# One layer on one core: attention scores from 32-bit terms in two halves of the array, in blocks of 2048 queries

## What is computed

```
xn  = layernorm(x)
q,k,v = xn @ Wq.T + bq, xn @ Wk.T + bk, xn @ Wv.T + bv     # 16 heads of 16
scores = (q * 16**-0.5) @ k.T                              # per batch and head: 4096 x 4096
attn = softmax(scores) @ v ;  attn @ Wo.T + bo
ffn(xn): 8 experts of width 256, silu(xn@Wg)*(xn@Wu) @ Wd, weighted by a router
out = x + attention + ffn
```

## Time and profile before

| | us |
|---|---|
| median of three launches | 7797.84 (7790.06 to 7806.21) |
| the profiled launch, span | 7797.1 |
| setup and tokens | 0 to 1378 |
| attention, first load to last column | 1378 to 7698 |
| output | 7699 to 7797 |

### The profile page before, as it was taken

How to read it: one execution, slowest core, us unless ns; L and a number is a source line. 1 busy time by engine, 2 the same in 40 slices (tenths; PEclk the granted TensorE clock), 3 DMA queues, 4 the chain that set the end, 5 groups by cost and what they waited for, 6 DMA issues and landing times. The chain is left out here.

```text
span 7797.1 us, 144290 instructions
## 1 busy us (share of the span) xinstructions
PE 7608.5 (98%) x42896; PEld 3174.4 (41%) x42896; DVE 5806.7 (74%) x7413; ACT 5255.3 (67%) x9557; POOL 542.1 (7%) x543
## 2 busy tenths in 40 slices
PE   7999999899999999999999999999999999999998
PEld 6888888233333333333333333333333333333334
DVE  5455454788787878787878787878787878787884
ACT  3333333577777777777777777777777777777774
POOL 2433333000000000000000000000000000000000
PEclk9999999899999999999999999999999999999999
DMA  2111110200000000000000000000000000000002
GB/s 75 42 42 34 41 42 28 62 8 8 8 8 8 8 8 8 8 8 8 8 8 8 8 8 8 8 8 8 8 8 8 8 8 8 8 8 8 8 0 86
DMA packets 97328, 135.88 MB, mean 17 GB/s; under 512 B 9824, under 2 KB 90976, under 8 KB 90976
## 3 DMA queue, kind: packets, MB, share of 16 engines
q1 hardware_dynamic: 97120, 133.48, 7.8%
HBM read 83.11 MB, written 50.33 MB: 17 GB/s over the span
## 5 line engine op out<-in xcount | busy, mean ns | idle before, releaser
L881 DVE TENSOR_REDUCE mx<-sc 128x1 f32<-128x1024 f32 x4096 | 4824.0, 1219 | 1138.4 <-PE sc L756 1138.4
L864 ACT ACTIVATE pr<-st 128x512 f32<-128x512 f32 x8160 | 4427.8, 595 | 1489.3 <-PE st L778 1375.2
L778 PE MATMUL st<-qr,kr 98*128 (+1 forms) x8160 | 2634.5, 387 | 75.3 <-ACT pr L864 51.8
L756 PE MATMUL sc<-kr,qr 96*128 (+1 forms) x8192 | 2140.5, 383 | 23.2 <-DMA kr<-parts_d 18.1
L785 PE MATMUL pv<-pr,vst 128*32 128x512 f32 x14336 | 1920.2, 608 | 0.1
L778 PEld LDWEIGHTS st<-qr,kr 98*128 98x128 bf16 x8160 | 648.6, 97 | 2469.5 <-ACT pr L864 2016.9
L756 PEld LDWEIGHTS sc<-kr,qr 96*128 (+1 forms) x8192 | 795.5, 97 | 1043.2 <-issue 141.3
L428 ACT ACTIVATE gated<-gate 128x512 f32<-128x512 f32 x256 | 152.3, 599 | 609.2 <-PE up L88 609.0
L613 DVE TENSOR_TENSOR hraw<-gated,up 128x512 f32<-128x512 f32 x256 | 173.3, 686 | 411.0 <-ACT gated L428 408.6
L785 PEld LDWEIGHTS pv<-pr,vst 128*32 128x32 f32 x14336 | 282.7, 108 | 416.9 <-issue 416.9
L724 POOL COPY vtail<-v_all 128x64 f32 (+1 forms) x32 | 7.6, 238 | 6074.8 <-PE pv L785 6074.8
(11 more groups left out here) (112 smaller groups left out, 2401.3 us busy)
## 6 DMA issues: line engine op xcount, KB each, us to landing
parts_d<-part SPq DMA_DIRECT2D x64, 384.0 KB, 2.7
qr<-parts_d SPq DMA_DIRECT2D x192, 128.0 KB, 4.3
kr<-parts_d SPq DMA_DIRECT2D x192, 128.0 KB, 7.0
x_in<-in_L_attn_hidden_states SPq DMA_DIRECT2D x16, 512.0 KB, 4.5
v_d<-v_sb SPq DMA_DIRECT2D x32, 256.0 KB, 2.1
base_d<-base SPq DMA_DIRECT2D x16, 512.0 KB, 3.2
v_all<-v_d SPq DMA_DIRECT2D x1, 8192.0 KB, 32.3
o_base<-base_d SPq DMA_DIRECT2D x16, 512.0 KB, 4.2
```

The source lines that it names most:

```text
L756: last = nc.tensor.matmul(sc[u % 2][:, j * GT:(j + 1) * GT], qr[0:ROWS, bass.ds(ring(stage) + qb * GT + t * P, P)], kr[0:ROWS, bass.ds(rin ...
L778: nc.tensor.matmul(score_bank(kb, maxima), kr[0:ROWSM, bass.ds(ring(stage) + kb * P, P)], qr[0:ROWSM, bass.ds(ring(stage) + qb * GT, GT)], ...
L864: nc.scalar.activation(pr[:, kb % PRING, :], score_bank(kb, maxima), ACT.Exp).then_inc(exp_done, 1)
L881: nc.vector.reduce_max(mx[:, odd, u // MAXU, u % MAXU:u % MAXU + 1], sc[u % 2][:, :], AX.X).then_inc(sc_read, 1)
```

## The change

**Parts.** q and k are split into two fp32r parts (high, low), not three bfloat16 ones. ACT writes the high part and DVE the low part straight from PE's bank; POOL has no part in it, and the separate full value is gone. The scale 1/4 is put into Wq in setup. `parts_d` holds float32, 512 KB a store.

**Scores.** A score is three terms (high-high, low-high, high-low), 48 rows, with two rows for the maximum 50. `load` puts the same rows at partitions 0 and at 64 of `qr` and `kr`, and two matmuls with different operands are issued behind each other, one in each half of the array: in `score_pair` two blocks of 512 queries against the same 128 keys, in `max_unit` the two halves of the 1024 keys. A load of one head is again 12 DMAs, now of 256 KB.

**Superslots.** One superslot is 2048 queries of a head (QH), 64 in all. For each of its 32 blocks of 128 keys (`kb`) PE issues two score pairs (four blocks of 128 by 512), two `max_unit` for the superslot after, and `times_v` of the block before: four float32 matmuls in the four column strips, one strip for each 512 queries. So one `kb` holds just what a quad held: 4 blocks of scores, 2 units of maxima, 4 products with v. The four strips are different queries now and need no adding. There are three banks `st` (STB), and a pair waits until the block three before its second member has been read. The maxima run a whole superslot and 16 units ahead (AHEAD).

**Maxima to rows.** Once in a superslot, after `times_v` at `kb` 26, PE transposes the 32 columns of maxima (`turned`) into a bank of `st`, ACT copies it to `mrow`, and four DMAs put it into the rows of `qr`.

**Results.** ACT copies `pv` to `oT` once in a superslot, and eight DMAs store sums and denominators, undivided and already feature by token, to `sums_d` and `den_d`. v of a head comes by one DMA from `v_d` in pieces of 16 numbers. The copies of v on POOL, `max_rows`, `out_back` and DVE's three steps after it are gone.

**Output.** The denominators are loaded, inverted by DVE and stored to `rden_d` first. Then SP issues for each group 2 loads of sums, 16 loads of one row of `rden_d` each, spread over 16 partitions, and the load of `base`. POOL multiplies the two. There are no transposes. The next group's loads wait for the store of the group before (`stored`) and for POOL (`attn_ready`).

**Loops.** The attention loop holds two heads, four superslots, written out in one body; the first and last pass stand outside it.

The diff, cut to this:

```diff
-UNITS = TPG * MAXU
-PAIRS = ((0, 0), (0, 1), (1, 0), (1, 1), (0, 2), (2, 0))
-ROWS = len(PAIRS) * HD
-ROWSM = ROWS + 2
+UNITS = QT * MAXU
+AHEAD = 16
+SUPERS = 2 * B * H
+TERMS = 3 * HD
+ROWSM = TERMS + 2
 VC = 32
-PRING = 2 * QUAD
+PRING = 16
+STB = 3
+SLOTS = KB * QSUB + 1
+ROWS_AT = 26
...
-                act.wait_ge(rest_ready, g * SPLITS + u + 1)
-                nc.scalar.activation(full[u % 2][:, :], bank[:, :], ACT.Identity, bias=bias[:, i:i + 1], scale=scale)
+                bias = c.bqs if kind == "q" else c.bk
                 act.wait_ge(parts_stored[u % 2], (g * (SPLITS // 2) + u // 2 + 1) * DMA)
-                nc.scalar.activation(part[u % 2][:, 0, :], bank[:, :], ACT.Identity, bias=bias[:, i:i + 1],
-                                     scale=scale).then_inc(misc_act, 1)
+                nc.scalar.activation(part[u % 2][:, 0, :], bank[:, :], ACT.Identity, bias=bias[:, i:i + 1]).then_inc(high_given, 1)
...
-                    dve.wait_ge(misc_act, g * MISC_ACT + emptied(n))
-                    dve.wait_ge(parts_ready, g * SPLITS + u + 1)
-                    nc.vector.tensor_tensor(rest[u % 2][:, :], full[u % 2][:, :], part[u % 2][:, 0, :],
-                                            ALU.subtract).then_inc(rest_ready, 1)
+                    bias = c.bqs if kind == "q" else c.bk
+                    dve.wait_ge(high_given, g * SPLITS + u + 1)
+                    nc.vector.scalar_tensor_tensor(out=part[u % 2][:, 1, :], in0=misc[(par * len(MISC) + n) % 2][:, :], scalar=bias[:, i:i + 1],
+                                                   in1=part[u % 2][:, 0, :].bitcast(F32), op0=ALU.add, op1=ALU.subtract).then_inc(misc_free, 1)
...
-        kr = sb("kr", [P, RING * S], BF16)
-        qr = sb("qr", [P, RING * S], BF16)
+        kr = [sb(f"kr{i}", [P, S], F32R) for i in range(RING)]
+        qr = [sb(f"qr{i}", [P, S], F32R) for i in range(RING)]
...
-        st = [pb(f"st{i}", [P, GT], F32) for i in range(2)]
+        st = [pb(f"st{i}", [P, GT], F32) for i in range(STB)]
-            load(0)
-            sp.dma_start(v_all[:, :, :], c.v_d.rearrange("(t p) d -> p t d", p=P)).then_inc(v_loaded, DMA)
-            sp.wait_ge(loaded, LOADS * DMA)
-            load(1)
-            with sp.Fori(RING, HEADS) as n:
-                wait_alone(sp, loaded, n * LOADS * DMA, passed)
-                wait_alone(sp, st_full, (n - RING + 1) * QB * KB, passed)
-                load(n)
+            def load(n, par):
+                for w, dst, order in ((0, qr, (0, 1, 0)), (1, kr, (0, 0, 1))):
+                    for grp in range(2):
+                        for term, hl in enumerate(order):
+                            r0 = 64 * grp + HD * term
+                            sp.dma_start(dst[par][r0:r0 + HD, :].bitcast(F32), c.parts_d[w, hl, bass.ds(n * HD, HD), :]).then_inc(qk_loaded, DMA)
+            def load_v(n, par):
+                sp.dma_start(vst[par][:, :, 0:HD],
+                             c.v_d[bass.ds((n // H) * S, S), bass.ds((n % H) * HD, HD)].rearrange("(t p) d -> p t d", p=P)).then_inc(v_loaded, DMA)
+            def rows(par, hf):
+                for grp in range(2):
+                    for hl in range(2):
+                        r = 64 * grp + TERMS + hl
+                        sp.dma_start(qr[par][r:r + 1, hf * QH:(hf + 1) * QH].bitcast(F32).rearrange("r (t q) -> r t q", q=P),
+                                     mrow[hl * QT:(hl + 1) * QT, :].bitcast(F32)).then_inc(rows_in, DMA)
+            def sums(s, n, hf):
+                wait_alone(sp, sums_ready, s + 2, passed)
+                for j in range(QSUB):
+                    cols = slice(hf * QH + j * GT, hf * QH + (j + 1) * GT)
+                    sp.dma_start(c.sums_d[bass.ds(n * HD, HD), cols], oT[VC * j:VC * j + HD, :]).then_inc(sums_stored, DMA)
+                    sp.dma_start(c.den_d[bass.ds(n, 1), cols], oT[VC * j + HD:VC * j + HD + 1, :]).then_inc(sums_stored, DMA)
...
-            def max_unit(n, u):
+            def max_unit(g, u, par, hf):
                 t, k = divmod(u, MAXU)
-                stage, qb = n // QB, n % QB
-                pe.wait_ge(sc_read, n * UNITS + u + 1)
-                for j in range(MAXW // GT):
-                    last = nc.tensor.matmul(sc[u % 2][:, j * GT:(j + 1) * GT],
-                                            qr[0:ROWS, bass.ds(ring(stage) + qb * GT + t * P, P)],
-                                            kr[0:ROWS, bass.ds(ring(stage) + k * MAXW + j * GT, GT)], start=True, stop=True)
+                q0 = hf * QH + t * P
+                pe.wait_ge(sc_read, g - 1 + SC_PRE)
+                for grp in range(2):
+                    r0, k0 = 64 * grp, k * MAXW + grp * GT
+                    last = nc.tensor.matmul(sc[u % 2][:, grp * GT:(grp + 1) * GT], qr[par][r0:r0 + TERMS, q0:q0 + P],
+                                            kr[par][r0:r0 + TERMS, k0:k0 + GT], start=True, stop=True)
...
-            def scores(stage, qb, kb, maxima):
-                n = (stage * QB + qb) * KB + kb
-                if maxima:
-                    pe.wait_ge(exp_done, n + 1)
-                elif qb == QB - LEAD and kb < 2:
-                    pe.wait_ge(exp_done, n + 1)
-                elif qb == QB - LEAD and kb < 4:
-                    pe.wait_ge(sc_read, HEADS * QB * UNITS + 2)
-                else:
-                    pe.wait_ge(exp_done, n - 1)
-                nc.tensor.matmul(score_bank(kb, maxima), kr[0:ROWSM, bass.ds(ring(stage) + kb * P, P)],
-                                 qr[0:ROWSM, bass.ds(ring(stage) + qb * GT, GT)], start=True, stop=True).then_inc(st_full, 1)
-            def times_v(quad, v, exps):
-                pe.wait_ge(exp_done, exps + 2)
-                for j in range(QUAD):
-                    last = nc.tensor.matmul(pv[VC * j:VC * (j + 1), :], v[:, j, :], pr[:, (quad % 2) * QUAD + j, :],
-                                            start=(quad == 0), stop=(quad == QUADS - 1))
+            def score_pair(s, kb, j0, par, hf, final):
+                x = slot_of(kb, j0, final)
+                pe.wait_ge(st_read, s * SLOTS + x + 1 - STB + 2 + READ_PRE)
+                for grp in range(2):
+                    r0, q0 = 64 * grp, hf * QH + (j0 + grp) * GT
+                    nc.tensor.matmul(st[(x + grp) % STB][:, :], kr[par][r0:r0 + ROWSM, kb * P:(kb + 1) * P],
+                                     qr[par][r0:r0 + ROWSM, q0:q0 + GT], start=True, stop=True).then_inc(st_full, 1)
+            def turned():
+                nc.tensor.transpose(st[ROWS_SLOT % STB][0:2 * QT, 0:P], nmp[:, :, :].rearrange("p h t -> p (h t)").bitcast(F32),
+                                    c.ident[:, :]).then_inc(st_full, 1)
+            def times_v(s, kb, par, final):
+                pe.wait_ge(st_read, s * SLOTS + slot_of(kb, QSUB - 1, final) + 2 + READ_PRE)
+                for j in range(QSUB):
+                    last = nc.tensor.matmul(pv[VC * j:VC * (j + 1), :], vst[par][:, kb, :], pr[:, (QSUB * kb + j) % PRING, :],
+                                            start=(kb == 0), stop=(kb == KB - 1))
...
+            for u in range(UNITS + 2):
+                max_unit(u, u % UNITS, 0, u // UNITS)
+            pe.wait_ge(max_chain, 3)
+            turned()
+            for u in range(UNITS + 2, UNITS + AHEAD):
+                max_unit(u, u % UNITS, 0, u // UNITS)
+            def body(i, first, last):
+                for q in range(PER):
+                    s, n, par, hf = PER * i + q, RING * i + q // 2, q // 2, q % 2
+                    ending = last and q // 2 == RING - 1
+                    for kb in range(KB):
+                        if kb == 0:
+                            pe.wait_ge(rows_in, (s + 1) * ROW_MOVES * DMA)
+                        if hf == 0 and not ending and 2 * kb + AHEAD == UNITS:
+                            pe.wait_ge(qk_loaded, (n + 2) * QK_LOADS * DMA)
+                        for half in range(2):
+                            score_pair(s, kb, 2 * half, par, hf, ending and hf)
+                            u = 2 * kb + AHEAD + half
+                            to = q + 1 + u // UNITS
+                            if not (last and to >= PER):
+                                max_unit(UNITS * (s + 1) + u, u % UNITS, to // 2 % RING, to % 2)
+                        if kb == 0:
+                            if not (first and q == 0):
+                                times_v(s - 1, KB - 1, par if hf else 1 - par, False)
+                            if hf == 0:
+                                pe.wait_ge(v_loaded, (n + 1) * DMA)
+                        else:
+                            if kb == 1:
+                                pe.wait_ge(sums_ready, s + 1)
+                            times_v(s, kb - 1, par, ending and hf)
+                        if kb == ROWS_AT and not (ending and hf):
+                            pe.wait_ge(max_chain, 3 * (s + 1) + 3)
+                            pe.wait_ge(st_read, s * SLOTS + ROWS_SLOT - STB + 2 + READ_PRE)
```

(79 more changed lines are left out.)

459 lines of the change are left out of this document (151 added, 308 removed).

## The result

The changed kernel took **7854.5 us** (median; 7836.2 to 7859.2) against 7798.7 for the kernel before in the same sessions: a ratio of 1.0067, with a 95% interval of 1.0053 to 1.0081. It is slower by 0.7%, where 7470 us and faster were forecast. The time is above the forecast's own 7150 to 7780 and inside the wider range to 8100, which took in a rival; the sign is wrong. The profiled launch is 7850.7 us long, 53.6 more than the one before. In a later session one of eight launches of the kernel before took 11802 us at a mean granted clock of 0.60, the others 7793 to 7801 us; the comparisons leave it out.

A forecast was written before the change was run, and what follows sets the result against it. A chain once through PE and once through ACT bounds it: 2.70 us a block for 2.88. Attention -562, opening +76, output +161, tokens -5 make -330 from 7797, say 7470 us; range 7150 to 7780, wider 7150 to 8100.

The forecast's parts named there:

- The chain's terms: Attention, one block of keys: 0.99 + 0.48 + 0.66 + 0.25 + 0.32 = 2.70 us, against 2.88 before.
- Pair to ACT: Attention chain, first score pair to ACT's exp: 0.43 plus 0.05 for the 32-bit weight load, 0.48 us.
- Second pair to the unit behind it: Attention chain, second score pair to the maxima behind it: halves run at once, so about one matmul, 0.25 us.
- rival 2: Attention: a pair's weight loads go in a row, 0.105 more for each of two pairs; block 2.90, total 7870 us; chance 0.12.
- Output: Output phase: 19 load issues a group at 0.50 us, 15.2 us a group, 259 us against 98.8: +161.
- Opening: First load to first score: fill 9, load 25, 80 units of maxima 94, in all 129 us against 52.7: +76.
- Tokens: Tokens and setup: PE stays the bound, only group 0's chain is shorter; -5 us, between -20 and +10.
- Last 40 blocks: End of attention: the last 40 blocks have no maxima, so 0.25 goes and each takes 2.45 us.
- Loop ends and superslots: Attention: pauses at 15 loop ends, 8 us each, 120; superslot extras 1.0 us x 63 = 63.
- 1 (halves not at once): Attention: the array's halves don't run at once, a pair costs 0.45, block 3.13, total 8330 us; chance 0.10.
- 3 (clock stays low): Attention: PE's clock stays at 0.50 throughout, block 4.12, +2850, total 10300 us; chance 0.04.
- 4 (DVE the bound): Attention: DVE's two reductions bound the block at 2.35 + 0.01 us, 680 less, total 6790 us; chance 0.03.

The follow-up runs named there:

- the reordered version: The changed kernel with both units of maxima between the two score pairs, instead of one between and one behind: 7335.3 us, ratio 0.9411.
- the fillers: Unread matmuls replace the last forty blocks' missing maxima, in the changed kernel with reordered maxima, reciprocals in two loads and add before split: 7181.9 us.
- both series runs: The changed kernel with both members of all score and maximum pairs, or of the maxima alone, at rows 0 to 63: 13254.6 and 11716.0 us.
- e4_few_issues: The changed kernel with a group's sixteen one-row loads of reciprocals in the output phase made two loads of eight rows: 7831.9 us, ratio 1.0035.
- e6_add_first: The changed kernel with DVE adding a group's result to base before it splits the next group in the output phase: 7808.8 us, ratio 1.0015.
- e2_bf16: The changed kernel with score and maximum matmuls reading only the upper 16 bits of each q and k number, as bfloat16: 7427.9 us.

## Why the prediction was wrong, point by point

- **What bounds the kernel**: right. The chain once through PE and once through ACT gave 2.88 before, and with its measured terms gives 2.84 after, 2.60 in the reordered version and 3.33 when both exps are waited for. ACT, DVE and PE each have time to spare in all of them.
- **The chain's terms**: this is the step that failed. `times_v` to pair 0.99: right. One exp instead of two: right, 0.49 by the run that put it back. Pair to ACT: 0.48, measured 0.54. Second pair to the unit behind it: 0.25, measured 0.34. Both hold the same error. I had the exposed load's price from the earlier trace rows, 0.105, but counted 0.05 for the first pair and nothing for the second, which waits for ACT too. 0.15 us x 2008 is 300 us. Alone it would have left 7767 us, still 30 under the kernel before; with the 80 us that the output missed the sign is turned. I had a case with 0.2 more a block, rival 2, but for another reason (loads in a row within a pair); the two loads of a pair start 3 or 4 ns apart and take 0.19 together, so that reason is wrong, and that its 7870 lies near the measured time is luck.
- **The unit behind the second pair** was charged right as to what it is, 0.25 given back, but I took it as part of the change. It was the cheapest thing to alter.
- **Output**: +161 forecast, +241 measured. The issues were nearly right (10.6 for 9.5); the wait of DVE's add behind the next group's split was missed, 6.8 us for 0.5.
- **Opening**: +76 forecast, +73 measured.
- **Tokens**: -5 forecast, +6 measured. PE was busy 594.5 of 600 us in the middle of the phase, as before (595.1), so the difference is at the two ends and in small parts; it was not tried further.
- **Last 40 blocks**: 2.45 forecast; 13 mostly at 2.67 and 27 at 4.13 measured, 151 us for 98: +53. The clock's part of it is shown by the fillers.
- **Loop ends and superslots**: 183 forecast. What is left of the steady part when 2008 blocks at 2.85 and the last 40 are taken off is 124. This is a remainder and not a measurement of its own.
- **Rivals**: 1 (halves not at once) is refuted. 3 (clock stays low) is not the changed kernel, but it is what both series runs did, for most of their time. 4 (DVE the bound) is not the changed kernel either, where DVE idles 0.44 us a block. The Trainium skill (TensorEngine Tiling (Array Packing), PSUM Bottleneck) says that tiling speeds up TensorE but not the reading of its results; here that bound would begin only some 0.24 us below the reordered version. The sign came from a sum of two mis-sized terms (0.15 a block and 5.9 us a group), neither of them a rival with a chance of its own. The block stayed just under the 2.86 that I had named as the point of loss, and the kernel lost all the same, because that point took the output's term as right.

The sum with measured terms: 7467 + 300 (chain) + 53 (last blocks) - 59 (loop ends) + 80 (output) + 11 (tokens) - 3 (opening) = 7849. The profiled launch is 7850.7. It had to come out so: the stretches are cut from that launch and the term of the loop ends is what was left over. It says where the time lies and is no second proof of the chain, for which the runs stand.

## What to carry to other kernels

When a matmul here waits for another engine, its weight load waits too (PEld idles 0.84 and 0.89 us before the pairs, released by ACT): price the load at every wait in the chain, not once, and by its type. Halving a matmul that lies beside something else gains nothing; ask of each one in a period whether it stands in the chain, and move those that don't belong there under the wait. In a pipelined store loop, look in which order an engine does this group's last step and the next group's first.

## What I had not expected of the hardware

- With all matmuls of scores and maxima in rows 0 to 63, the clock stayed at 0.50 for over 11 ms, with PE busy 11356.7 of 11370 us. With only the maxima there, it was at 0.50 for 1413 us from the opening on, then at 1.00 for 396, and at 0.50 again for 8223. The changed kernel, with the same work in two halves and gaps in PE's time, came back each time. The Trainium skill (TensorE: Matmul & The Clock Gate, Why this matters for your kernels) says to keep TensorE busy continuously for the full clock; here continuous work did not bring it, and the measurement decides.
- That the rows are the cause is not shown. Each of the two kernels was launched once, and the kernel before, which uses rows 0 to 97, did nearly the same in one of 32 launches on record, the one of 11802 us: by its mean clock of 0.60 it was at 0.50 for some 9.4 of 11.8 ms. It has no trace here. None of the 33 launches of the changed kernel and of those variants of it that keep the two halves did so. More launches of the series kernels could tell. The opening's own stretch at 0.50 differs between launches too: 140 us in the changed kernel, 249 in e4_few_issues and e6_add_first, whose attention phase is the same code.
- In the last superslot the clock fell to 0.50 while PE went on working, and it stayed there with PE busy 88.9 of 110 us; extra matmuls in its gaps held it at 1.00 and brought 47 us.
- A 32-bit weight load of 128 columns costs some 0.10 us more at the head of a waiting matmul than a 16-bit one (e2_bf16), and two loads into different halves go together: 0.19 for both.
